# A transformer block on one core: the order of work on four engines and the order of users in a ring of seven PSUM banks are changed

## The chip, the cores and the metric

The kernel runs on one core of a Trainium2 chip. The metric is the device time of one execution, in microseconds. TensorE (PE), VectorE (DVE), ScalarE (ACT), GpSimd (POOL) and the DMA queue of SyncE (SP) run side by side and meet only at semaphores.

## The reference, cut to what matters

The input is 8 sequences of 256 tokens with 128 features. A stack of six layers runs twice with the same weights, with a selective-scan layer between the two. Everything is float32.

```
for i in range(6):
    x = attn_layer(shift_tokens(x), Wqkv[i], q_scale[i], k_scale[i], Wo[i]) + x
    x = ffn_layer(shift_tokens(x), ln_g[i], ln_b[i], W1[i], b1[i], W2[i], b2[i]) + x
```

attn_layer projects to queries, keys and values (16 heads of 64), divides queries and keys by their norms, rotates both (rotary tables), takes scores in windows of 32 queries against the 64 keys of the window and the one before it, adds a mask, takes the softmax, sums the values and projects back to 128 features. ffn_layer is a layer norm, a gated GELU layer with 341 hidden features, and a projection back.

## The kernel before, in words

**Items and steps.** The 8 sequences are 4 chunks of 2 (128 x 512 elements). An item is one chunk in one layer, so each stack has 24 items. An item is spread over some 29 steps, and a new item starts every 8 steps, so that about four items are always in work. A step takes one pair of heads of the newest item through its projections. Below, "step 0" to "step 7" means the step number modulo 8. Every engine walks the same list PLAN, and inside each step it does its own pieces in an order written out by hand (`tensor_stack`, `vector_stack`, `scalar_stack`, `gpsimd_stack`). An engine never looks ahead: what stands first waits, and the rest waits behind it.

**What falls where.** In every step: PE projects queries (L659 to L661, into "proj 0"), keys (the same lines, "proj 1") and the previous pair's values (L752 to L754); ACT squares queries and keys (L1096); DVE multiplies them by sine and cosine tables (L881, L886; "rotate 0" and "rotate 1") and turns the values (L902); SP moves the sine part across partitions; POOL adds it (L1270). In even steps, for one group of four heads: PE scores (L722, 128 small matmuls) and the spread of the inverse key norms (L741); ACT masks (L1148), key norms copied (L1154), exponents (L1173), attention output copied (L1166); DVE scaled scores (L951, one instruction for each of two sequences), sum (L963), reciprocal (L968), maximum (L957); POOL softmax division (L1290); PE the value product (L695, 128 small matmuls). In odd steps: POOL takes off the maximum (L1276) and scales (L1284); DVE turns the probabilities (L977). Once an item: first half of the output projection and gates in step 1 (L671, L762; DVE L915; norm work DVE L933, L935, L938 and then ACT L1132), value part of the hidden layer in steps 2 and 3 (L767, DVE L984), its projection in step 4 (L774, DVE L991), second half of the output projection in step 5 (L671, DVE L915), then the token shift on ACT (L1079, L1080), centering in step 6 (PE L637, ACT L1062, POOL L1248), variance in step 7 (PE L642, DVE L847). In step 6 the next item's tokens are split in a high and a low part (ACT L1111 xs_hi, DVE L908 xs_lo). At the end of a layer the next layer's weights are split pair by pair (ACT L1103, POOL L1295).

**The bank ring.** PE writes into 7 general PSUM banks that are handed out in turn by `Banks.use`. Each user waits until the reader of the bank's last user has signalled; as there are 7 banks, that is the user seven places earlier. One period of 8 steps has 63 uses, which is nine turns of the ring, so every item finds the same pattern. In an even step the uses before the change are: proj 0, spread, scores of sequence 0, scores of sequence 1, (a use of the once-an-item work), proj 1, four of the value product, v. The readers' signals are cos_q and cos_k (DVE L886), k_inv_kept (ACT L1154), k_norms_off (DVE L951), att_kept (ACT L1166), v_kept (DVE L902).

**Masks.** Scores are added onto a mask that is already in the bank. Where the bank's last user had written it whole, ACT copies the mask in; otherwise PE writes it with a matmul (L712):

```
if BANKS.filled[key]:
    w.wait_ge(S["mask_set"], MASKED[key])
else:
    pe_bank(w, key)
    e.matmul(g[seq][:, :], ident_bf[:, :], mask_bf[:, :], start=True, stop=False, skip_group_check=True)
```

The value product does not write its banks whole; the projections, v, the spread and the scores do.

## Time and profile before

| | |
|---|---|
| median of 3 runs | 3372.07 us (3358.28 to 3372.07) |
| the profiled execution's own time | 3364.97 us |
| its span | 3363.2 us |
| mean granted clock of TensorE | 0.946 of full speed |
| busy: PE / DVE / ACT / POOL | 86% / 87% / 61% / 72% of the span |

A row of a timeline gives start, duration, engine, line, operation, output<-inputs, and in brackets the engine's idle time before it and what released it. Rows of groups give count, busy time and mean duration, then idle time before them with the releasers. A busy PE is one whose matmuls are in flight, not one at its peak. "issue" is idle time in which the engine waited for nothing that the profile shows.

### The profile page before, as it was taken

The page shows a single profiled execution, that of the slowest core. Times are in us where ns is not written, and L with a number is a line of the kernel's source. Part 1 is how long each engine was busy: PE and PEld are TensorE (multiplying, and loading weights), DVE is VectorE, ACT ScalarE, POOL GpSimd, SP SyncE. Part 2 cuts the span into 40 slices and gives each one's busy share as a digit, 9 for nine tenths or more (in the row PEclk, how much of TensorE's full clock was granted, in tenths as well). Part 3 has the DMA queues.
Part 4 walks back from the last instruction along what each step waited for, and adds up shares of the span by engine and source line. Part 5 has one row for each costly group of instructions (what it writes and reads, how often), then busy time and mean ns, then how long its engine had stood idle before and what let it go on. Part 6 is the DMA issues. An engine that isn't in the chain of part 4 may idle for free. (4 is left out here: it accounts for less than half of the span.)

```text
span 3363.2 us, 132089 instructions
## 1 busy us (share of the span) xinstructions
PE 2891.1 (86%) x57914; PEld 1829.9 (54%) x57914; DVE 2933.3 (87%) x4224; ACT 2059.8 (61%) x3820; POOL 2423.5 (72%) x1679
## 2 busy tenths in 40 slices
PE   5689988988999989897677788999998989998987
PEld 3455555655666655553233455555565555555553
DVE  6789989999999988986898789889899989898984
ACT  3466666666676666665663566666566666566663
POOL 3678787787787787874464678778787787787773
PEclk8899999999999999998897899999999999999998
DMA  5233333333333333320002233333343333342330
GB/s 136 65 80 77 82 91 74 84 92 71 84 92 73 89 85 72 88 65 28 10 4 59 68 81 78 75 93 77 73 101 73 86 90 71 82 94 65 88 74 15
DMA packets 114726, 250.85 MB, mean 75 GB/s; under 512 B 27244, under 2 KB 60648, under 8 KB 114152
## 3 DMA queue, kind: packets, MB, share of 16 engines
q1 hardware_dynamic: 114152, 242.40, 30.5%
q8 instruction: 457, 7.49, 1.0%
q14 instruction: 117, 0.96, 0.1%
HBM read 37.82 MB, written 3.15 MB: 12 GB/s over the span
## 5 line engine op out<-in xcount | busy, mean ns | idle before, releaser
L1096 ACT ACTIVATE squares<-general 128x512 f32<-128x512 f32 x768 | 453.7, 597 | 716.8 <-PE general L661 707.8
L1290 POOL TENSOR_TENSOR probs<-probs,row_sum 128x1024 f32<-128x1024 f32 x192 | 365.4, 1903 | 442.4 <-DVE row_sum L968 442.3
L1270 POOL TENSOR_TENSOR q_ring<-q_ring,partner 128x512 f32<-128x512 f32 x384 | 491.0, 1279 | 203.9 <-DMA partner<-sines 203.3
L881 DVE TENSOR_TENSOR sines<-general,layer_tables 128x512 f32<-128x512 f32 x768 | 515.8, 672 | 85.3 <-ACT squares L1096 81.8
L1270 POOL TENSOR_TENSOR k_ring<-k_ring,partner 128x512 f32<-128x512 f32 x384 | 490.9, 1278 | 0.0
L695 PE MATMUL general<-probs_t,v_buf 32*64 32x64 f32 x24576 | 339.0, 234 | 153.8 <-issue 85.1
L659 PE MATMUL general<-xs_hi,wqkv_lo 128*128 128x512 f32 x768 | 454.2, 591 | 18.5 <-DVE xs_lo L908 8.0
L695 PEld LDWEIGHTS general<-probs_t,v_buf 32*64 32x64 f32 x24576 | 304.0, 134 | 246.1 <-issue 237.5
L1284 POOL TENSOR_TENSOR probs<-probs,q_scale 128x1024 f32<-128x1024 f32 x192 | 365.4, 1903 | 15.1
L722 PE MATMUL general<-k_ring,q_ring 64*32 64x64 f32 (+1 forms) x24576 | 295.3, 223 | 92.5 <-issue 53.1
L671 PE MATMUL general<-att,wo 128*128 128x512 f32 x768 | 366.2, 621 | 4.6 <-ACT att L1166 4.2
L1276 POOL TENSOR_TENSOR probs<-probs,row_max 128x1024 f32<-128x1024 f32 x192 | 366.7, 1910 | 0.0
L722 PEld LDWEIGHTS general<-k_ring,q_ring 64*32 64x32 f32 x24576 | 261.1, 105 | 126.8 <-issue 109.4
L661 PE MATMUL general<-xs_hi,wqkv_hi 128*128 128x512 f32 x768 | 313.1, 408 | 2.3 <-issue 2.2
L660 PE MATMUL general<-xs_lo,wqkv_hi 128*128 128x512 f32 x768 | 313.1, 408 | 1.9 <-issue 1.9
L659 PEld LDWEIGHTS general<-xs_hi,wqkv_lo 128*128 128x128 f32 x768 | 152.1, 198 | 267.9 <-issue 235.5
L1166 ACT ACTIVATE att<-general 128x256 f32<-128x256 f32 x768 | 231.4, 388 | 93.0 <-PE general L695 92.6
L902 DVE STREAM_TRANSPOSE v_buf<-general 128x512 f32<-128x512 f32 x384 | 264.8, 690 | 25.4 <-PE general L754 25.2
L733 PE MATMUL sums<-squares,consts 128*32 128x512 f32 x1536 | 249.0, 612 | 38.8 <-ACT squares L1096 36.5
L963 DVE TENSOR_REDUCE row_sum<-probs 128x16 f32<-128x1024 f32 x192 | 230.2, 1199 | 52.2 <-ACT probs L1173 51.8
L951 DVE TENSOR_TENSOR probs<-general,k_inv 128x512 f32<-128x512 f32 x384 | 244.8, 677 | 29.7 <-PE general L722 27.7
L752 PE MATMUL general<-xs_hi,wqkv_lo 128*128 128x256 f32 x768 | 258.7, 337 | 3.5 <-issue 3.5
(233 smaller groups left out, 6369.9 us busy)
## 6 DMA issues: line engine op xcount, KB each, us to landing
partner<-sines SPq DMA_DIRECT2D x1536, 128.0 KB, 2.3
wqkv_raw<-in_wqkv SPq DMA_DIRECT2D x80, 208.0 KB, 2.7
wo<-in_wo SPq DMA_DIRECT2D x12, 512.0 KB, 5.1
w<-in_w SPq DMA_DIRECT2D x12, 341.0 KB, 3.2
base_dram<-x SPq DMA_DIRECT2D x8, 256.0 KB, 2.4
att<-in_wqkv SPq DMA_DIRECT2D x2, 1024.0 KB, 6.7
sines<-base_dram SPq DMA_DIRECT2D x8, 256.0 KB, 3.9
w<-in_w SPq DMA_DIRECT2D x12, 128.0 KB
```

The source lines that it names most:

```text
L659: e.matmul(g[:, :], wqkv_lo[:, p, cut], xs_hi[:, r, :], start=True, stop=False)
L660: e.matmul(g[:, :], wqkv_hi[:, p, cut], xs_lo[:, r, :], start=False, stop=False)
L661: e.matmul(g[:, :], wqkv_hi[:, p, cut], xs_hi[:, r, :], start=False, stop=True)\
L671: done = e.matmul(g[:, :], wo[:, p, :], att[:, p, :], start=(p == OUT_PAIRS[i][0]), stop=(p == OUT_PAIRS[i][-1]))
L695: done = e.matmul(o, lhs, rhs, start=(kb == 0), stop=True, skip_group_check=True)
L722: done = e.matmul(o, qw, kw, start=False, stop=True, skip_group_check=True)
L881: e.tensor_tensor(by_seq(sines[:, i % 2, which, :]), g, both(layer_tables[:, 2 * which + 1, :]), ALU.mult).then_inc(S[f"sin_{side}"], 1)
L1096: e.activation(squares[:, (2 * p + which) % 4, :], general_of(("proj", k, n, p, which))[:, :], ACT.Square).then_inc(S[f"squared_{side}"], 1)
L1270: e.tensor_tensor(y, y, partner[:, i % 2, which, :], ALU.add).then_inc(S[f"rotated_{side}"], 1)
L1276: e.tensor_tensor(y, y, spread_keys(row_max[:, i % 2, :]), ALU.subtract).then_inc(S["max_off"], 1)
L1284: e.tensor_tensor(y, y, spread_keys(q_scale8[:, n % 2, group, :]), ALU.mult).then_inc(S["q_norms_off"], 1)
L1290: e.tensor_tensor(y, y, spread_keys(row_sum[:, i % 2, :]), ALU.mult).then_inc(S["probs_done"], 1)
```

## The change

No arithmetic is added or removed. The lags become plain numbers with the same values. What moves:

- **Ring and PE, even steps:** the uses are now proj 0, scores 0, scores 1, spread; on PE the spread stands between the two halves of the scores (windows 0 to 3 and 4 to 7). First half of the output projection and variance also stand ahead of the scores in the text, but they fall in odd steps, which have no scores.
- **Ring and PE, step 4:** the keys' projection (proj 1) now comes before the hidden layer's output projection. The same holds for the entering norms of the first items. The value product's halves are no longer separated by the second output projection, which falls in an odd step.
- **DVE:** the turn of the probabilities ahead of rotate 1 (odd steps); in step 1 the addition of the first output half (L915) ahead of the norm work (L933, L935, L938).
- **ACT:** weight splitting (L1103) to the front of the step; layer-norm root ahead of the queries' squares (step 0); exponents ahead of the keys' squares (even steps); in step 6 the centering copy (L1062) ahead of the token split (L1111).
- **POOL:** the softmax division behind the second addition of the rotary parts.
- Separate names in `Step` for the pieces on different engines, with the same step numbers as before.

```
 # Banks.stack
-            if st.spread:
-                n, group = st.spread
-                self.use(("spread", k, n, group), "k_inv_kept", (g + n) * GROUPS + group + 1)
...
             if st.scores:
                 n, group = st.scores
                 for seq in range(CHUNK_SEQS):
                     self.use(("scores", k, n, group, seq), "k_norms_off", ((g + n) * GROUPS + group) * 2 + seq + 1)
...
+            if st.spread:
+                n, group = st.spread
+                self.use(("spread", k, n, group), "k_inv_kept", (g + n) * GROUPS + group + 1)
```

```
 # tensor_stack
                 if st.now:
                     pe_project(e, w, k, *st.now, 0)
...
+                if st.scores:
+                    pe_scores(e, w, k, *st.scores, range(0, NWIN // 2))
                 if st.spread:
                     pe_spread(e, w, k, *st.spread)
-                if st.out_first:
-                    pe_out(e, w, k, *st.out_first)
-                if st.scores:
-                    pe_scores(e, w, k, *st.scores, range(0, NWIN // 2))
...
-                if st.ffn_out is not None:
-                    pe_ffn_out(e, w, k, st.ffn_out)
...
+                if st.now:
+                    pe_project(e, w, k, *st.now, 1)
+                if st.ffn_out is not None:
+                    pe_ffn_out(e, w, k, st.ffn_out)
                 if st.enter:
                     pe_enter(e, w, k, *st.enter)
-                if st.now:
-                    pe_project(e, w, k, *st.now, 1)
```

```
 # vector_stack
-                if st.norms_back is not None:
-                    dve_norms_back(e, w, k, st.norms_back)
...
-                if st.out_first:
-                    dve_out(e, w, k, *st.out_first)
+                if st.first_added is not None:
+                    dve_out(e, w, k, st.first_added, 0)
...
+                if st.norms_back is not None:
+                    dve_norms_back(e, w, k, st.norms_back)
+                if st.turn:
+                    dve_turn(e, w, k, *st.turn)
                 if st.now:
                     dve_rotate(e, w, k, *st.now, 1)
-                if st.turn:
-                    dve_turn(e, w, k, *st.turn)
```

```
 # scalar_stack
+                if st.exps:
+                    act_exp(e, w, k, *st.exps)
...
-                if st.split is not None:
-                    act_split_tokens(e, w, k, st.split)
...
                 if st.center is not None:
                     act_center(e, w, ("ffn", k, st.center))
+                if st.split is not None:
+                    act_split_tokens(e, w, k, st.split)
...
                 if st.now:
                     act_square(e, w, k, *st.now, 1)
-                if st.exps:
-                    act_exp(e, w, k, *st.exps)
```

```
 # gpsimd_stack
-                if st.exps:
-                    pool_probs(e, w, k, *st.exps)
                 if st.enter:
                     pool_enter(e, w, k, *st.enter)
                 if st.added:
                     pool_rotate(e, w, k, *st.added, 1)
+                if st.probs:
+                    pool_probs(e, w, k, *st.probs)
```

## Rows read from the trace of the kernel before

**Rows 1.** Windows: length, busy us (instructions) by engine, TensorE clock, DMA share, GB/s

```profile
400.00:1300.00 900.00, 814.64 (x17666) 530.76 (x17664) 823.52 (x1201) 581.58 (x1100) 706.41 (x488) 0.98 0.36 83
1094.00:1154.00 60.00, 56.51 (x1207) 36.21 (x1205) 56.91 (x84) 39.67 (x75) 48.24 (x33) 1.00 0.39 93
839.00:842.00 3.00, 3.00 (x8) 1.92 (x8) 2.42 (x4) 0.60 (x1) 1.49 (x1) 0.53 0.22 52
```

**Rows 2.** Groups by line: busy us, mean ns, idle before and its releasers

```profile
L902 DVE STREAM_TRANSPOSE v_buf<-general 128x512 f32<-128x512 f32 x384 | 264.8, 690 | 25.4 <-PE general L754 25.2
...
L963 DVE TENSOR_REDUCE row_sum<-probs 128x16 f32<-128x1024 f32 x192 | 230.2, 1199 | 52.2 <-ACT probs L1173 51.8
...
L1295 POOL TENSOR_TENSOR wqkv_lo<-wqkv_raw,wqkv_hi 128x416 fp32r<-128x416 f32 x80 | 87.9, 1099 | 57.3 <-ACT wqkv_hi L1103 57.3
...
L915 DVE TENSOR_TENSOR x<-x,general 128x512 f32<-128x512 f32 x96 | 64.2, 669 | 68.5 <-PE general L671 68.5
...
L712 PE MATMUL general<-mask_bf,ident_bf 128*128 128x512 bf16 x18 | 6.0, 386 | 0.0
```

**Rows 3.** Source line L991, once an item: count, first and last start

```profile
L991 DVE SCALAR_TENSOR_TENSOR x<-general,vec,x x19: 724/729/751, 299.5 to 1397.9; 128x512 f32<-128x512 f32 x19
```

**Rows 4.** Timeline of DVE over one undisturbed item: its two second output additions bound it

```profile
1097.11 0.69 DVE L915 TENSOR_TENSOR x<-x,general 128x512 f32<-128x512 f32 x1 [1.18 <-PE general L671]
...
1103.30 0.68 DVE L908 TENSOR_TENSOR xs_lo<-xs,xs_hi 128x512 fp32r<-128x512 f32 x1
1104.33 0.69 DVE L881 TENSOR_TENSOR sines<-general,layer_tables 128x512 f32<-128x512 f32 x1 [0.35 <-ACT squares L1096]
...
1132.71 1.27 DVE L951 TENSOR_TENSOR probs<-general,k_inv 128x512 f32<-128x512 f32 x2
...
1136.19 1.22 DVE L963 TENSOR_REDUCE row_sum<-probs 128x16 f32<-128x1024 f32 x1 [0.36 <-ACT probs L1173]
...
1154.60 0.69 DVE L915 TENSOR_TENSOR x<-x,general 128x512 f32<-128x512 f32 x1 [1.16 <-PE general L671]
```

**Rows 5.** Timeline of PE, same item

```profile
1100.39 1.53 PE L722 MATMUL general<-k_ring,q_ring 64*32 64x32 f32 x128 [0.48 <-ACT general L1148]
...
1111.40 0.39 PE L741 MATMUL general<-inv_parts,spread_sel 128*128 128x256 f32 x2
1111.73 1.46 PE L722 MATMUL general<-k_ring,q_ring 64*32 64x32 f32 x128
...
1115.44 0.41 PE L695 MATMUL general<-probs_t,v_buf 32*64 32x64 f32 x19 [1.35 <-DVE q_ring L886]
...
1129.91 1.49 PE L722 MATMUL general<-k_ring,q_ring 64*32 64x32 f32 x128 [0.53 <-ACT general L1148]
...
1133.53 1.23 PE L695 MATMUL general<-probs_t,v_buf 32*64 32x64 f32 x94 [0.37 <-DVE probs L951]
```

**Rows 6.** Timeline of ACT, same item

```profile
1099.12 1.12 ACT L1148 ACTIVATE general<-mask_bf 128x512 f32<-128x512 bf16 x2
...
1101.24 0.63 ACT L1111 ACTIVATE xs_hi<-xs 128x512 fp32r<-128x512 f32 x1
1103.01 0.60 ACT L1062 ACTIVATE centered<-general 128x512 f32<-128x512 f32 x1 [1.14 <-PE general L637]
...
1128.13 0.63 ACT L1132 ACTIVATE inv_parts<-k_inv 128x512 fp32r<-128x512 f32 x1 [1.07 <-DVE k_inv L938]
```

**Rows 7.** Timeline of POOL, same item, steps 6 and 2

```profile
1103.68 1.19 POOL L1248 TENSOR_TENSOR rstd<-centered 128x512 f32<-128x512 f32 x1 [0.49 <-ACT centered L1062]
...
1135.12 1.29 POOL L1270 TENSOR_TENSOR q_ring<-q_ring,partner 128x512 f32<-128x512 f32 x1 [3.46 <-DMA partner<-sines]
```

**Rows 8.** Timeline of DVE in step 6 of an item at a layer's end

```profile
982.69 1.81 DVE L908 TENSOR_TENSOR xs_lo<-xs,xs_hi 128x512 fp32r<-128x512 f32 x1
```

**Rows 9.** Timeline of POOL at the same time

```profile
982.68 1.28 POOL L1270 TENSOR_TENSOR k_ring<-k_ring,partner 128x512 f32<-128x512 f32 x1
```

**Rows 10.** Timeline of PE in step 2 of an earlier, disturbed item

```profile
838.34 0.35 PE L753 MATMUL general<-xs_lo,wqkv_hi 128*128 128x256 f32 x1 [2.15 <-issue]
```

More of the change, by code:

```diff
@@ L34 @@
 POOL_BANKS = 7
[L37 to L45 removed]
+SCORES_LAG = 10
+SCORES_REST_LAG = 10
+SCALE_LAG = 10
+OFF_LAG = 11
+EXP_LAG = 12
+PROBS_LAG = 12
+TURN_LAG = 13
+VALUES_LAG = 14
+VALUES_REST_LAG = 14
+KEPT_LAG = 14
 V_LAG = 1
[L47 removed]
+SPREAD_LAG = 10
 PROBS = 2
@@ L108, in __init__ @@
         self.exps = self.group(t, EXP_LAG)
+        self.probs = self.group(t, PROBS_LAG)
         self.turn = self.group(t, TURN_LAG)
@@ L275, in stack @@
                 self.use(("proj", k, n, p, 0), "cos_q", (g + n) * PAIRS + p + 1)
-            if st.spread:
-                n, group = st.spread
-                self.use(("spread", k, n, group), "k_inv_kept", (g + n) * GROUPS + group + 1)
-            if st.out_first:
-                n, i = st.out_first
-                self.use(("project", k, n, i), "att_added", (g + n) * 2 + i + 1)
+            if st.out_first is not None:
+                self.use(("project", k, st.out_first, 0), "att_added", (g + st.out_first) * 2 + 1)
+            if st.var is not None:
+                self.var(("ffn", k, st.var))
             if st.scores:
@@ L285, in stack @@
                     self.use(("scores", k, n, group, seq), "k_norms_off", ((g + n) * GROUPS + group) * 2 + seq + 1)
-            if st.var is not None:
-                self.var(("ffn", k, st.var))
+            if st.spread:
+                n, group = st.spread
+                self.use(("spread", k, n, group), "k_inv_kept", (g + n) * GROUPS + group + 1)
             if st.center is not None:
                 self.norm(("ffn", k, st.center))
-            if st.ffn_out is not None:
-                self.use(("ffn_out", k, st.ffn_out), "ffn_added", g + st.ffn_out + 1)
             if st.gates is not None:
@@ L298, in stack @@
                     self.use(("value", k, n, j), "hidden_done", (g + n) * 3 + j + 1)
+            if st.now:
+                n, p = st.now
+                self.use(("proj", k, n, p, 1), "cos_k", (g + n) * PAIRS + p + 1)
+            if st.ffn_out is not None:
+                self.use(("ffn_out", k, st.ffn_out), "ffn_added", g + st.ffn_out + 1)
             if st.enter and st.enter[1] == 0:
@@ L302, in stack @@
                 self.var(("enter", k, st.enter[0]))
-            if st.now:
-                n, p = st.now
-                self.use(("proj", k, n, p, 1), "cos_k", (g + n) * PAIRS + p + 1)
             if st.values:
```

99 lines of the change are left out of this document (49 added, 50 removed).

## The prediction, made before the changed kernel had run

> **What bounds the kernel now.** I read the windows first. In the steady stretch from 400 to 1300 us DVE is busy 823.5 of 900 us and PE 814.6, while POOL (706) and ACT (582) have room [rows 1]. No single engine is the bound: DVE and PE each have about 9% idle time, and the question is who makes whom wait. An item comes every (1397.9 - 299.5) / 18 = 61.0 us [rows 3]. Items without a disturbance are shorter: from one second output addition to the next it is 1154.60 - 1097.11 = 57.5 us [rows 4], at a full clock [rows 1]. The other 3.5 us are stalls of PE that the profile gives to nothing, such as 2.15 us in [rows 10], and the stretches of lower clock behind them [rows 1].
>
> The timelines of the undisturbed item show that the path changes engine twice an item. In step 5 DVE waits 1.18 and, an item later, 1.16 us for PE's second half of the output projection [rows 4]; all items together wait 68.5 us there, 48 second halves, 1.43 each [rows 2]. So PE is late at that point in every item. Going back along PE, it works without a wait worth naming to the value product of step 2, which starts at 1133.53, 0.14 us after the first of DVE's two scaled-score instructions ends (1132.71 + 0.68 = 1133.39), and which the trace puts down to it [rows 5]. This is the ring: the fourth bank of that product is the one in which the scores of sequence 0 stood, seven uses before. From there back, the path is on DVE to the output addition in step 5, with no idle over 0.2 us but the 0.35 at 1104.33. One item is thus a **DVE leg** (step 5 to step 2) and a **PE leg** (step 2 to step 5). What shortens a wait of DVE inside the PE leg gains nothing; DVE waits longer in step 5 instead. That holds for the 0.36 us before the row sum at 1136.19 [rows 4] and for most of the 51.8 us before all row sums [rows 2].
>
> **The change part by part, in us an item.**
>
> *Gate of the value product.* In an even step the uses before were proj 0, spread, scores 0, scores 1; in step 2 the fourth bank of the product came from scores 0, the third from the spread. With the spread behind the scores the same two banks come from scores 1 and scores 0. The product must now wait for DVE's second scaled-score instruction: 1133.98 instead of 1133.39. That moves the start of the PE leg by **0.6**. In step 0 there is no once-an-item use in between, and the gate moves from cos_q (the 1.35 us wait at 1115.44, [rows 5]) to the first scaled scores, again 0.6 later. In an undisturbed item PE has slack behind it (it waits 0.53 for masks at 1129.91); in a disturbed item, where PE arrives late at step 2, this one counts instead. So 0.6 either way; bounds 0 and 1.2.
>
> *Centering copy ahead of the token split, step 6.* ACT made xs_hi at 1101.24, while it waited 1.14 us for PE's centering [rows 6], and DVE could make xs_lo at 1103.30 and go on at 1104.33 [rows 4]. Now ACT first waits: centered 1103.01 to 1103.61, xs_hi to about 1104.25, then xs_lo (0.68) on DVE, with the second rotation queued behind it, and behind that the row sum, the values' turn and the whole DVE leg. The rotation starts near 1104.9 instead of 1104.33. Two things move it. PE's centering comes about 0.1 earlier: the wait of 0.48 for two masks [rows 5] is nearly gone, since here one mask becomes a PE matmul, but the spread (0.33) and that matmul (6.0 / 18 = 0.33, [rows 2]) come in. Against it stands POOL: its square runs from 1103.68 to 1104.87 [rows 7], over the new place of xs_lo. Where xs_lo began together with a POOL addition it took 1.81 us instead of 0.68 [rows 8, 9], the addition's 1.28 and its own work. If that holds here, the rotation starts near 1105.4. So 0.5 or 1.0. In disturbed items DVE waits for PE later in the step anyway (25.2 us before L902, [rows 2]) and takes up a part. I take **0.7**; bounds 0.2 and 1.1.
>
> The Trainium skill ("SBUF — State Buffer", "SBUF: two separate sides") says that a VectorE instruction with both inputs in SBUF and a GpSimd instruction that reads SBUF exclude each other for a whole instruction, whoever starts first. Rows 8 and 9 agree. By it alone the term would be 1.0 and the time some 13 us more; the chosen value stands between.
>
> *Spread inside the scores.* PE changes between the full array and small tiles twice more a group. The spread takes 0.33 us from its start to that of the scores [rows 5], with one change in it; nothing shows a change alone, so it costs between 0 and 0.33, and as the two matmuls must take the larger part, about 0.1. One group (step 4) lies in the PE leg: **0.2**; bounds 0 and 0.66.
>
> *Output addition ahead of the norm work, step 1.* inv_parts (1128.13, [rows 6]) comes 0.65 later, behind it the masks and scores of step 2 (1129.91), and the spread is no longer done in that wait. PE then reaches the value product of step 2 some 1.1 later: it had 0.37 to spare [rows 5] and gets 0.6 more from the new gate. **0.1**; bounds 0 and 0.5.
>
> *The rest, taken at nothing.* Keys' projection ahead of the hidden output (step 4): both stand in the PE leg, in the other order; DVE adds the hidden output before it rotates, so its start differs by 0.3 at most, covered by the 1.16 wait in step 5. Exponents ahead of the keys' squares: ACT mostly idles there, and the exponents' input is a step old; in step 0 a table load and the exponents now stand before the squares, while DVE still has the turn of the root to do; where that cover is too short, DVE's second rotation starts late, by 0 to the 0.69 of its first instruction [rows 4]. Turn ahead of rotate 1: the sum is the same, but the sine part of the keys is 1.23 later in odd steps, so SP's four transfers too, and POOL's next addition, which waited 3.46 for them already [rows 7] with nothing of the path behind it. Division behind the second addition on POOL: it waited for DVE's reciprocal anyway, and the turn that needs it is a step later. Masks: about 92 fewer on ACT, as many matmuls on PE at 0.33, in steps 6 (counted) and 0 (PE has the 1.35 wait). Weight splits at the front of ACT's step: POOL waited 57.3 us for 16 of them [rows 2], beside the path mostly; I give it **-5 us in all**, bounds -20 and 5.
>
> *Sum.* 0.6 + 0.7 + 0.2 + 0.1 = 1.6 an item. Of 48 items about 42 have full neighbours: 67 us, less 5. The profiled execution took 3364.97 (span 3363.2), which gives 3427; the runs' median is 7 us above it, and I forecast **3430**.
>
> **Rivals.**
>
> *Faster: DVE alone sets the pace.* If the output wait in step 5 were made by DVE's own lateness, each wait taken from DVE would count, first the 51.8 us before the row sums: 3365 - 52 = 3313. For it: DVE is busy longer than PE. Against it: the 1.43 us in every item, and the value product pinned to DVE 0.14 us behind. It decides if that wait in step 5 shrinks under about 0.3 us while step 2 starts no later. 0.19.
>
> *No change.* The disturbances (3.5 us an item) hide the 0.6 and the 0.7 instead of adding to them, as where DVE waits for PE's values. 3355 to 3388, at 3372. For it: 27 such waits. Against it: a stall of PE inside the PE leg adds to a later start. 0.14.
>
> *Slower still: the clock.* PE's wait of 1.35 before the value product of step 0 grows by 0.6, and by what DVE loses in step 6, to about 2.7 us. Behind a gap of 2.15 [rows 10] the granted clock was 0.53, which is the lower level of 1.2 GHz [rows 1], while in the undisturbed item, gaps of 1.35 included, it was 1.00. The 3 us window at 0.53 did about 1.4 us less work than one at 2.4 GHz; with some 0.3 to 0.5 of it taken up by PE's slack, 1.1 more for 42 items: 3430 + 46 = 3476. 0.15. The Trainium skill ("TensorE: Matmul & The Clock Gate", "HAM oscillation — how this bites in real kernels") warns that idle gaps between groups of matmuls put the clock back down; that is this rival.
>
> **How the numbers follow.** The forecast has 0.52; its own range from the terms' bounds is 3385 to 3475. The rivals have 0.19, 0.14 and 0.15. A measurement of this kernel can tell about 0.5%, 17 us. Faster: 0.20, same 0.14, slower 0.66. The range 3345 to 3480 leaves out most of the faster rival (0.13) and the upper part of the clock rival (0.07).
>
> **What would show it.** (1) The value product of steps 2, 4 and 6 starts no earlier than the second L951 of its step, that of step 0 no earlier than the first. (2) In step 6 xs_lo starts only behind the centering copy, at times with a duration above 0.68, and the keys' sine after it starts 0.5 to 1 later. (3) The row sum waits for the exponents almost never, and the wait in step 5 before L915 grows from 1.2 to about 1.7. (4) L712 rises to some 110, L1148 falls to some 274. (5) POOL's wait before L1295 is gone. I am wrong if an undisturbed item takes under 58 us, most likely because DVE's earlier row sums carry through to step 5, or if the clock falls in step 0.

## The result, and the profile after

The changed kernel takes 3424.01 us (median of 4 runs, 3416.67 to 3424.89) where the kernel before takes 3371.48 in the same session: a ratio of 1.0161, 95% interval 1.0132 to 1.0189. The forecast was 3430. The profiled execution has a span of 3422.9 us, 59.7 more than before.

Where those 59.7 us are is seen in one line that stands once an item. The addition of the hidden output to x, 24 times a stack, first and last start (L991 before, L1000 after). The kernel before, first stack, then second:

```profile
L991 DVE SCALAR_TENSOR_TENSOR x<-general,vec,x x24: 724/732/751, 235.7 to 1644.6; 128x512 f32<-128x512 f32 x24
L991 DVE SCALAR_TENSOR_TENSOR x<-general,vec,x x24: 723/728/751, 2007.1 to 3357.6; 128x512 f32<-128x512 f32 x24
```

The changed kernel, first stack, second stack, and last the stretch that answers to [rows 3]:

```profile
L1000 DVE SCALAR_TENSOR_TENSOR x<-general,vec,x x24: 734/751/752, 217.2 to 1680.3; 128x512 f32<-128x512 f32 x24
L1000 DVE SCALAR_TENSOR_TENSOR x<-general,vec,x x24: 750/751/752, 2024.9 to 3417.3; 128x512 f32<-128x512 f32 x24
L1000 DVE SCALAR_TENSOR_TENSOR x<-general,vec,x x19: 750/751/752, 281.3 to 1424.6; 128x512 f32<-128x512 f32 x19
```

The first of them comes 18.5 us **earlier**. The 23 items behind it take 54.2 us more. From the last of stack 0 to the first of stack 1 it is 344.6 us instead of 362.5, so 17.9 less, and then 41.9 more. The sum is -18.5 + 54.2 - 17.9 + 41.9 = 59.7. So the steady part lost 96 us and the fillings of the pipeline gained 36. The item takes (1424.6 - 281.3) / 18 = 63.5 us instead of 61.0. The shortest item, from one second output addition to the next, takes 60.0 us instead of 57.5. The prediction had 1.6 for the item and nothing for the start.

The windows of the changed kernel: the stretch of the first line of [rows 1], one item, and three microseconds behind the value product of step 0 in it:

```profile
400.00:1300.00 900.00, 816.24 (x16950) 521.11 (x16949) 803.00 (x1153) 548.82 (x1032) 683.33 (x471) 0.95 0.34 80
805.00:866.00 61.00, 56.07 (x1168) 35.84 (x1154) 55.62 (x81) 37.49 (x71) 43.61 (x30) 0.97 0.31 71
823.00:826.00 3.00, 3.00 (x67) 2.81 (x54) 2.93 (x5) 1.21 (x4) 2.83 (x3) 0.50 0.32 72
```

DVE does 48 instructions fewer in the same 900 us, PE 716 fewer. The groups that answer to [rows 2], and those of the small operations that turn out to matter, in the changed kernel:

```profile
L911 DVE STREAM_TRANSPOSE v_buf<-general 128x512 f32<-128x512 f32 x384 | 268.5, 699 | 30.5 <-PE general L763 30.3
L972 DVE TENSOR_REDUCE row_sum<-probs 128x16 f32<-128x1024 f32 x192 | 229.5, 1195 | 6.0 <-ACT probs L1182 6.0
L924 DVE TENSOR_TENSOR x<-x,general 128x512 f32<-128x512 f32 x96 | 65.7, 684 | 103.9 <-PE general L680 103.8
L858 DVE TENSOR_SCALAR norm_t<-norm_t 128x16 f32<-128x16 f32 x56 | 52.2, 932 | 1.9
L917 DVE TENSOR_TENSOR xs_lo<-xs,xs_hi 128x512 fp32r<-128x512 f32 x48 | 50.9, 1061 | 39.1 <-ACT xs_hi L1120 39.1
L1000 DVE SCALAR_TENSOR_TENSOR x<-general,vec,x 128x512 f32<-128x512 f32 x48 | 36.0, 751 | 69.3 <-PE general L783 69.3
L704 PE MATMUL general<-probs_t,v_buf 32*64 32x64 f32 x24576 | 345.7, 244 | 199.5 <-DVE probs L960 124.9 <-issue 69.1 <-DVE v_buf L911 3.3
L1304 POOL TENSOR_TENSOR wqkv_lo<-wqkv_raw,wqkv_hi 128x416 fp32r<-128x416 f32 x80 | 90.6, 1133 | 8.0 <-ACT wqkv_hi L1112 8.0
L721 PE MATMUL general<-mask_bf,ident_bf 128*128 128x512 bf16 x110 | 41.6, 390 | 7.0 <-ACT general L1157 7.0
```

The same four groups in the kernel before:

```profile
L849 DVE TENSOR_SCALAR norm_t<-norm_t 128x16 f32<-128x16 f32 x56 | 20.4, 364 | 1.9
L908 DVE TENSOR_TENSOR xs_lo<-xs,xs_hi 128x512 fp32r<-128x512 f32 x48 | 43.1, 897 | 0.0
L991 DVE SCALAR_TENSOR_TENSOR x<-general,vec,x 128x512 f32<-128x512 f32 x48 | 35.4, 737 | 31.3 <-PE general L774 31.1
L695 PE MATMUL general<-probs_t,v_buf 32*64 32x64 f32 x24576 | 339.0, 234 | 153.8 <-issue 85.1 <-DVE q_ring L886 53.2 <-DVE probs L951 6.4
```

The row sums no longer wait (51.8 to 6.0). The output additions wait 35 us more, but not where the prediction had it: 21 of the 35 lie before the first halves in step 1, which never waited before. Before the second half in step 5 the wait is 1.13 us in the median instead of 1.16, and 1.36 in the mean instead of 1.13. The value product waits for the scaled scores and no longer for the cosine, and 121.9 of these 124.9 us lie in step 0. From the views of line L695 before and L704 after, what the product waited for, us and times:

```profile
  DVE q_ring L886: 53.2, 33
  DVE probs L951: 6.4, 17
```

```profile
  DVE probs L960: 124.9, 46
```

The split of the tokens waits for ACT, which it never did. And **L858**, an in-place addition to 16 numbers a partition, takes 932 ns instead of 364. The prediction did not name it.

**Step 7, where it shows.** Timeline of DVE in step 7 of one item of the changed kernel:

```profile
815.13 0.70 DVE L856 STREAM_TRANSPOSE norm_t<-general 128x512 f32<-128x512 f32 x1
815.87 0.95 DVE L858 TENSOR_SCALAR norm_t<-norm_t 128x16 f32<-128x16 f32 x1
816.86 0.26 DVE L860 RECIPROCAL norm_t<-norm_t 128x16 f32<-128x16 f32 x1
```

Timeline of POOL at the same time, and in step 1 of the next item:

```profile
814.88 1.90 POOL L1285 TENSOR_TENSOR probs<-probs,row_max 128x1024 f32<-128x1024 f32 x1
816.86 1.91 POOL L1293 TENSOR_TENSOR probs<-probs,q_scale 128x1024 f32<-128x1024 f32 x1
...
830.04 1.90 POOL L1285 TENSOR_TENSOR probs<-probs,row_max 128x1024 f32<-128x1024 f32 x1
832.02 1.91 POOL L1293 TENSOR_TENSOR probs<-probs,q_scale 128x1024 f32<-128x1024 f32 x1
```

DVE in that step 1:

```profile
830.88 1.15 DVE L942 CAST norm_t<-norm_t 128x128 fp32r<-128x128 f32 x1
832.06 2.01 DVE L944 TENSOR_TENSOR norm_t<-norm_t 128x128 f32<-128x128 f32 x1
```

POOL's subtraction ends at 816.78 and L858 at 816.82; the next pair ends at 831.94 and L942 at 832.03; the one after at 833.93 and L944 at 834.07. Each of the three DVE operations ends just behind a POOL operation that was running when it began. In the kernel before, POOL had its second rotary addition first in these steps and the subtraction started 1.2 us later. The reciprocal L860 starts together with the next POOL operation and takes 0.26 all the same, and the transposition L856 runs under the subtraction in 0.70. So it is certain forms of operation that are shut out. The views by line, durations in ns (min/median/max), the addition before, then the addition and the reciprocal after:

```profile
L849 DVE TENSOR_SCALAR norm_t<-norm_t x56: 181/334/1566, 18.8 to 3342.3; 128x16 f32<-128x16 f32 x56
L858 DVE TENSOR_SCALAR norm_t<-norm_t x56: 182/956/1434, 18.4 to 3402.3; 128x16 f32<-128x16 f32 x56
L860 DVE RECIPROCAL norm_t<-norm_t x56: 255/256/259, 18.6 to 3402.5; 128x16 f32<-128x16 f32 x56
```

In both traces the four additions that met no POOL operation took 0.18 us. All 47 that began under the subtraction in the changed kernel ended 0.04 us behind it. In the kernel before, 44 began under a rotary addition and ended 0.04 us behind that, so the 0.33 there was partly such a wait too. L944 is held in both kernels (1832 ns in the mean before, 1784 after): what changed for it is the POOL operation behind which it ends, the scaling instead of the subtraction. The Trainium skill ("SBUF — State Buffer", "SBUF: two separate sides") says that a VectorE instruction that has two SBUF inputs and a GpSimd instruction that reads SBUF exclude each other for a whole instruction, and so do a VectorE instruction in a mode that uses two ports and a GpSimd instruction. The three rows of L858, L942 and L944 fit it; that L858 and L942, with one tensor input, are in such a mode is not shown by any row.

**Steps.** A step is here the time between two queries' sines (L881, L890). Medians over the 38 items with full neighbours in both stacks, in us; then the mean item (over the 36 of them that are followed by such an item), and the time that the first three items take together, in the first stack and in the second. Each row is one profiled execution. All experiments are listed, for use below.

| | 0 | 1 | 2 | 3 | 4 | 5 | 6 | 7 | mean item | first three |
|---|---|---|---|---|---|---|---|---|---|---|
| before | 9.21 | 8.42 | 8.50 | 5.46 | 7.60 | 6.22 | 7.87 | 5.37 | 61.3 | 171.4, 169.3 |
| changed | 9.18 | 8.56 | 8.19 | 5.46 | 8.77 | 5.98 | 8.64 | 5.98 | 63.4 | 153.5, 150.8 |
| split_first | 9.19 | 8.57 | 8.19 | 5.46 | 8.72 | 5.98 | 7.90 | 6.00 | 62.7 | 153.8, 154.0 |
| division_between | 9.20 | 7.88 | 8.20 | 5.46 | 8.80 | 5.98 | 8.69 | 5.37 | 61.8 | 163.3, 162.3 |
| spread_first | 9.19 | 8.56 | 7.72 | 5.46 | 8.45 | 6.19 | 8.60 | 5.99 | 62.4 | 156.6, 155.2 |
| norms_first | 9.19 | 9.16 | 8.01 | 5.46 | 8.92 | 5.98 | 8.63 | 5.99 | 63.4 | 156.4, 150.9 |
| turn_back | 9.19 | 8.57 | 7.90 | 5.46 | 8.72 | 5.98 | 8.63 | 5.98 | 62.9 | 155.9, 154.2 |
| ffn_first | 9.20 | 8.57 | 8.03 | 5.46 | 8.83 | 6.00 | 8.65 | 5.99 | 63.5 | 154.4, 154.0 |
| no_epsilon | 9.21 | 8.56 | 8.19 | 5.46 | 8.72 | 5.98 | 8.64 | 4.99 | 62.1 | 154.9, 153.3 |
| before, exps_early | 9.21 | 8.42 | 7.29 | 5.46 | 8.45 | 6.22 | 7.69 | 5.37 | 61.0 | 168.4, 165.2 |
| before, division_last | 9.20 | 9.16 | 8.47 | 5.46 | 7.50 | 6.22 | 7.77 | 5.99 | 62.2 | 160.5, 157.9 |
| three_back | 9.21 | 7.83 | 7.90 | 5.46 | 8.40 | 6.19 | 7.77 | 5.37 | 61.1 | 161.3, 160.6 |
| three_back_start | 9.21 | 7.83 | 7.71 | 5.46 | 8.44 | 6.19 | 7.88 | 5.37 | 61.3 | 157.1, 153.2 |
| three_back_start_ffn | 9.21 | 7.83 | 7.78 | 5.46 | 8.44 | 6.22 | 7.80 | 5.37 | 61.1 | 155.3, 153.1 |

### The profile page after: what moved, and what is told of

Its sections match the earlier page's. It is cut to its first block, busy times and chain, and to the rows that moved or that the text cites. A ratio compares the mean times of both kernels' runs of the same rounds, so it can differ in the third digit from the quotient of the medians.

```text
span 3422.9 us, 132096 instructions
## 1 busy us (share of the span) xinstructions
PE 2988.4 (87%) x58006; PEld 1860.0 (54%) x58006; DVE 2978.5 (87%) x4224; ACT 2020.2 (59%) x3728; POOL 2428.4 (71%) x1679
## 4 chain that ended last, share of the span: by engine, by line
PE 57%; DVE 24%; issue 9%; ACT 5%; POOL 2%; DMA 1%; SPq 1%; DVEq 0%; POOLq 0%; ACTq 0%
PE general L680 8%; PE general L704 7%; PE general L731 7%; PE general L668 4%; PE sums L742 4%; PE general L776 4%; PE general L783 4%; PE general L669 3%; PE general L670 3%; DVE sines L890 3%; PE general L761 3%; PE general L771 2%; PE general L750 2%; PE general L762 2%; DVE q_ring L895 2%
## 5 line engine op out<-in xcount | busy, mean ns | idle before, releaser
L890 DVE TENSOR_TENSOR sines<-general,layer_tables 128x512 f32<-128x512 f32 x768 | 512.3, 667 | 61.0 <-ACT squares L1105 57.6
L704 PE MATMUL general<-probs_t,v_buf 32*64 32x64 f32 x24576 | 345.7, 244 | 199.5 <-DVE probs L960 124.9
L704 PEld LDWEIGHTS general<-probs_t,v_buf 32*64 32x64 f32 x24576 | 313.4, 142 | 308.7 <-issue 306.2
L668 PE MATMUL general<-xs_hi,wqkv_lo 128*128 128x512 f32 x768 | 438.6, 571 | 16.3 <-DVE xs_lo L917 7.6
L731 PE MATMUL general<-k_ring,q_ring 64*32 64x64 f32 (+1 forms) x24576 | 330.4, 223 | 43.1 <-issue 22.3
L761 PE MATMUL general<-xs_hi,wqkv_lo 128*128 128x256 f32 x768 | 273.1, 356 | 5.7 <-issue 5.5
L895 DVE TENSOR_TENSOR q_ring<-general,layer_tables 128x512 f32<-128x512 f32 x384 | 259.8, 677 | 0.0
```

The source lines that it names most:

```text
L668: e.matmul(g[:, :], wqkv_lo[:, p, cut], xs_hi[:, r, :], start=True, stop=False)
L704: done = e.matmul(o, lhs, rhs, start=(kb == 0), stop=True, skip_group_check=True)
L731: done = e.matmul(o, qw, kw, start=False, stop=True, skip_group_check=True)
L761: e.matmul(g[:, cut], wqkv_lo[:, p, cols], xs_hi[:, r, cut], start=seq == 0, stop=False, skip_group_check=True)
L890: e.tensor_tensor(by_seq(sines[:, i % 2, which, :]), g, both(layer_tables[:, 2 * which + 1, :]), ALU.mult).then_inc(S[f"sin_{side}"], 1)
```

## The experiments

All times are given as ratios to the kernel before on the same chip and in the same session; 0.1% is 3.4 us. The changed kernel's own ratio, 1.0161, is from the first session, so that a difference to it is known to some 0.4% (14 us), and the error of 1.0161 is in every such difference. The kernel before had a median of 3371.48 us in that session and of 3359.66, 3357.31 and 3368.96 in the later ones. Unless it says "before", an experiment is the changed kernel with one edit.

**Token split ahead of the centering copy (split_first).**

```
+ if st.split is not None: act_split_tokens(...)
  if st.center is not None: act_center(...)
- if st.split is not None: act_split_tokens(...)
```

> The changed kernel with one order put back: ScalarE makes the rounded tokens ahead of the centering copy again (step 6). In the trace of the changed kernel the keys' sine of step 6 starts 4.54 us into the step against 3.43 before, and the token split of VectorE lasts 1.11 us, under GpSimd's square. Theory (every delay of VectorE between step 5 and step 2 is on the path): step 6 gets back 0.7 to 1.1 us, times 42 items, so 29 to 46 us faster than the changed kernel: 3378 to 3395, ratio to the kernel before 1.002 to 1.007. Rival (disturbances or another engine take the item's end anyway): the time stays at 3424, ratio 1.015, with the sine earlier all the same.

Measured: 1.0094 (1.0062 to 1.0126), 23 us faster than the changed kernel's 1.0161. Step 6 is back to 7.90, and the split, in the groups of this kernel, is no longer stretched or waited for:

```profile
L917 DVE TENSOR_TENSOR xs_lo<-xs,xs_hi 128x512 fp32r<-128x512 f32 x48 | 33.9, 706 | 5.3 <-ACT xs_hi L1120 5.2
```

The gain is clear of the rival's nothing, and under the theory's 29 to 46 us. The delay of step 6 is on the path.

**Division between the two rotary additions (division_between).**

```
  pool_rotate(..., 0)
+ if st.probs: pool_probs(...)
  if st.enter: pool_enter(...)
  pool_rotate(..., 1)
- if st.probs: pool_probs(...)
```

> The changed kernel with GpSimd's division of the probabilities back between its two rotary additions, ahead of its part of the entering norm. In the changed kernel GpSimd's subtraction of the row maximum starts 0.94 us into step 7 instead of 2.17 and VectorE's small addition of the variance lasts 0.95 us instead of 0.33 under it; step 7 grew from 5.37 to 5.98 us. Theory A (the earlier subtraction blocks VectorE, and step 7 is in the VectorE leg): the small addition is back at 0.33, step 7 at about 5.4, 0.6 x 42 = 25 us faster, ratio about 1.008. Part of it may be lost again in the first items of each stack, where the changed kernel gained some 18 us a stack: if the place of the division behind the entering norm is what gave that, the first three items lose up to 36 us together and the time is no shorter, ratio 1.016 to 1.02. Rival B (step 7 grew for another reason): no change in step 7, ratio 1.016.

Measured: 1.0076 (1.0049 to 1.0102), 29 us faster. Step 7 gave 0.61 as theory A said, and step 1 gave 0.68, which it did not say. Against that the first three items lost 9.8 and 11.5 us. The small operations of step 7 on DVE, then the groups of the two that the subtraction had stretched, in this kernel:

```profile
802.72 0.34 DVE L858 TENSOR_SCALAR norm_t<-norm_t 128x16 f32<-128x16 f32 x1
803.09 0.26 DVE L860 RECIPROCAL norm_t<-norm_t 128x16 f32<-128x16 f32 x1
```

```profile
L858 DVE TENSOR_SCALAR norm_t<-norm_t 128x16 f32<-128x16 f32 x56 | 20.4, 365 | 1.9
L942 DVE CAST norm_t<-norm_t 128x128 fp32r<-128x128 f32 x48 | 31.0, 647 | 3.6 <-ACT norm_t L1135 3.4
```

**Spread ahead of the scores (spread_first).**

```
  pe_project(..., 0)
+ if st.spread: pe_spread(...)
  pe_out(..., 0); pe_var(...); pe_scores(..., range(0, NWIN // 2))
- if st.spread: pe_spread(...)
  pe_scores(..., range(NWIN // 2, NWIN))
```

with the same move in Banks.

> The changed kernel with the spread ahead of the scores (and of the first half of the output projection) again, on TensorE and in the ring of banks. Theory: the bank gate of the value products goes back from the second to the first scaled-score instruction (0.6 us earlier in steps 2, 4 and 6, and to the queries' cosine in step 0), and the two changes between full array and small tiles vanish (0.2): 0.8 us of an item, 30 to 35 us, ratio 1.005 to 1.008. Rival (PE's slack behind the gate takes the 0.6, so that only the 0.2 shows): 8 us, ratio 1.013. Rival (the gate matters more, since it also brings the low clock behind the wait of step 0): 50 us or more, ratio about 1.00, and the granted clock of the whole run back at 0.946 from 0.932.

Measured: 1.0069 (1.0040 to 1.0099), 31 us faster, inside the theory's range. Steps 2 and 4 fall by 0.47 and 0.32, step 5 rises by 0.21. Where in those steps it lies is another matter than the theory had it. The product of step 2 starts 2.66 us into the step instead of 2.69, so hardly earlier; the keys' sine of that step, whose projection PE makes ahead of the product, starts 3.40 us into it instead of 3.73. In step 4 the product starts at 3.39 instead of 3.74, and the hidden output ahead of it is earlier by as much. The value product waits for the cosine again:

```profile
L704 PE MATMUL general<-probs_t,v_buf 32*64 32x64 f32 x24576 | 346.3, 241 | 186.0 <-DVE q_ring L895 97.6 <-issue 80.8 <-DVE v_buf L911 4.2
```

The last rival fell in both halves: 31 us and not 50, and the clock of the run stays at 0.936.

**The kernel before, exponents early alone (exps_early).**

```
  act_norms(...)
+ if st.exps: act_exp(...)
  ...
  act_square(..., 1)
- if st.exps: act_exp(...)
```

> The kernel before with one edit alone: ScalarE's exponents ahead of the rest of its step (behind the norms), so ahead of the keys' squares. Theory (the waits that VectorE has before its row sums, 52 us in all, lie mostly inside TensorE's leg and are given back in the wait of step 5; but steps 6 and 0 are in VectorE's own leg): -15 to +5 us, ratio 0.996 to 1.002, the row-sum wait almost gone and the wait before the second output addition up from 68.5 us. Rival (VectorE alone sets the pace): 52 us faster, ratio 0.985. Rival (the table load and the exponents ahead of the keys' squares delay the second rotation): 10 to 25 us slower, ratio 1.003 to 1.007.

Measured: 0.9941 (0.9908 to 0.9975), 20 us faster, a little more than the theory's range and far from the 52. Step 2 loses 1.21 us, and step 4 takes back 0.85. Of the 44 us that the row sums no longer wait, 21 reappear before the sines, which wait for the squares of PE's projections, and 4 each before the output additions and the additions of the hidden output (31.3 to 35.4). The sines' group in the kernel before:

```profile
L881 DVE TENSOR_TENSOR sines<-general,layer_tables 128x512 f32<-128x512 f32 x768 | 515.8, 672 | 85.3 <-ACT squares L1096 81.8 <-DMA partner<-sines 1.2
```

The groups of this kernel:

```profile
L881 DVE TENSOR_TENSOR sines<-general,layer_tables 128x512 f32<-128x512 f32 x768 | 517.5, 674 | 105.9 <-ACT squares L1096 101.5 <-DMA partner<-sines 0.6
L963 DVE TENSOR_REDUCE row_sum<-probs 128x16 f32<-128x1024 f32 x192 | 229.8, 1197 | 7.6 <-ACT probs L1173 7.5
L915 DVE TENSOR_TENSOR x<-x,general 128x512 f32<-128x512 f32 x96 | 64.2, 669 | 72.8 <-PE general L671 72.8
```

**The three orders back together (three_back).**

> The changed kernel with three orders put back together: the token split ahead of the centering copy on ScalarE, GpSimd's division between its two rotary additions, the spread ahead of the scores. Alone they gave ratios to the kernel before of 1.0094, 1.0076 and 1.0069, from 1.0161: 0.67%, 0.85% and 0.92% each. Theory (VectorE's leg and TensorE's leg follow one another in every item, so what is taken from either adds up): the sum, 2.4%, ratio 0.992 (3335 us where the kernel before takes 3362), an item of 60.1 us in the steady part. Rival (they cover one another: once VectorE is early, TensorE's leg or its disturbances set the time, or the reverse): not below 1.000, an item of 61.3 us or more. The long wait of the second output addition tells them apart: by the theory it stays near 1.4 us an item.

Measured: 0.9924 (0.9892 to 0.9955), 2.4% under the changed kernel, the sum of the three. That sum holds the error of 1.0161 three times and is known to 1% only, so it excludes the rival (not below 1.000) but cannot show that the three add up in full. The medians of the steps add up as well: 0.7 (split) + 1.2 (division) + 0.6 (spread) is 2.5, and the sum over the steps falls from 60.76 to 58.13, 2.6. But the mean item is 61.1, not 60.1: of the 3.3 us that it lost in the three single runs, 2.3 came. In part that is made up in the first items, where the three together lose 7.8 and 9.8 us and the single runs sum to 13 and 19. The wait of the second output addition, by which the two theories were to be told apart, has a mean of 1.13 us in step 5, as in the kernel before, against 1.36 in the changed kernel. What disturbs the items in this kernel I did not separate.

**The kernel before, division last alone (division_last).** The reverse of the second experiment, on the other kernel.

> The kernel before with one edit alone: GpSimd's division of the probabilities behind its second rotary addition. Theory (the subtraction of the row maximum starts 1.2 us earlier in the odd steps and shuts VectorE's small two-input or in-buffer operations out while it runs): step 7 +0.6 us (the variance's small addition 0.95 instead of 0.33) and step 1 +0.6 us (in the norm work, an operation that read 0.5 to 1.0 takes 1 to 2), 1.2 x 42 = 50 us slower in the steady part, less up to 20 in the first three items of each stack: ratio 1.009 to 1.015. Rival (the division's place costs only together with the other edits): 1.000, steps 7 and 1 at 5.37 and 8.42 us as before.

Measured: 1.0095 (1.0057 to 1.0133), 32 us slower. Step 7 is at 5.99, step 1 at 9.16. This one edit has the two signs of the whole: an item 0.9 longer and the first three items 10.9 and 11.4 us shorter. The groups of this kernel:

```profile
L849 DVE TENSOR_SCALAR norm_t<-norm_t 128x16 f32<-128x16 f32 x56 | 53.7, 959 | 1.9
L933 DVE CAST norm_t<-norm_t 128x128 fp32r<-128x128 f32 x48 | 66.9, 1394 | 25.3 <-ACT norm_t L1126 25.3
```

**Norm work ahead of the first output addition (norms_first)**, on DVE: the call of dve_norms_back back in front of the output addition.

> The changed kernel with VectorE's norm work (three operations, step 1) ahead of the first output addition again. The prediction costed this edit at 0.1 us an item. In the trace of the changed kernel the addition waits up to 3.2 us for TensorE's first half in the disturbed items, with the norm work queued behind it; in undisturbed items it does not wait. Theory (that wait is now in VectorE's leg): with the norm work ahead the wait is filled, 1 to 2 us in a third of the items, 15 to 30 us faster than the changed kernel, ratio 1.007 to 1.012. Rival (the addition later means the second half, the scores of step 2 and the gate behind them are no earlier, so nothing comes of it): 1.015 to 1.018.

Measured: 1.0205 (1.0178 to 1.0232). The gain that the theory forecast did not come. Against the changed kernel's 1.0161 this is 0.44% more, at the edge of the 0.4% to which such a difference is known, and the times themselves (3422.15 against 3424.01) and the mean items (63.4 in both) are equal. So no difference between the two kernels is shown. Step 1 is 9.16 instead of 8.56, and step 2 behind it is shorter, 8.01 instead of 8.19. The wait of the output addition did shrink, but the norm work now waits for ACT's root, and its operations begin nearer to the start of POOL's subtraction:

```profile
L942 DVE CAST norm_t<-norm_t 128x128 fp32r<-128x128 f32 x48 | 59.3, 1235 | 33.0 <-ACT norm_t L1135 32.6
L944 DVE TENSOR_TENSOR norm_t<-norm_t 128x128 f32<-128x128 f32 x48 | 90.3, 1881 | 1.7
L924 DVE TENSOR_TENSOR x<-x,general 128x512 f32<-128x512 f32 x96 | 64.2, 669 | 75.1 <-PE general L680 75.1
```

The output addition, which reads a PSUM bank, keeps its time under the subtraction (676 to 689 ns in all 96 of the changed kernel), so it is the better one to have there for step 1; for the whole item nothing is gained.

**Turn behind the second rotation (turn_back)**, on DVE.

> The changed kernel with VectorE's turn of the probabilities behind the second rotation again. The prediction took this edit at nothing: the same work in both orders, only the keys' sine 1.2 us later with the turn ahead. Theory: ratio 1.014 to 1.018, as the changed kernel, with GpSimd's second addition starting 1 us earlier and no step of VectorE shorter. Rival (the later sine, the four transfers behind it and GpSimd's addition push the rest of GpSimd's step, and so the subtraction and scaling that the exponents wait for): 10 to 25 us faster, ratio 1.009 to 1.013. The other side (the turn earlier lets the value products start earlier): slower, ratio 1.02 or more.

Measured: 1.0146 (1.0113 to 1.0180). The interval holds the changed kernel's ratio, as the theory has it, and also the end of the rival's range (1.013); the mean item is 62.9 instead of 63.4. No difference is shown, and one of 10 us is not excluded.

**Hidden output ahead of the keys' projection (ffn_first)**, on PE and in Banks.

> The changed kernel with TensorE's hidden output ahead of the keys' projection again (step 4), on TensorE and in the ring of banks. The prediction took this order at nothing. In the changed kernel step 4 grew from 8.1 and 7.4 us (medians of the two stacks) to 8.8 and 8.7, and VectorE's addition of the hidden output, now behind both projections, waits for TensorE 69 us in all against 31. Theory (both stand in TensorE's leg, so the order only moves the wait between steps 4 and 5): step 4 0.4 shorter, step 5 longer by as much, ratio 1.013 to 1.018. Rival (the late hidden output holds VectorE's second rotation, which the values and the output projection do not need, but the steps behind do): 0.5 us an item, 21 us faster, ratio 1.008 to 1.012.

Measured: 1.0166 (1.0138 to 1.0195): nothing. The total is as the theory had it, the steps are not: step 4 did not get shorter (8.83 against 8.77) nor step 5 longer. The hidden output's addition waits 41.7 us instead of 69.3, but the sines of step 4 now wait for their squares instead, 27.7 us against 3.4, and the output additions still wait 104.0:

```profile
L1000 DVE SCALAR_TENSOR_TENSOR x<-general,vec,x 128x512 f32<-128x512 f32 x48 | 36.0, 749 | 41.7 <-PE general L783 41.4
```

**Without the small addition (no_epsilon).** The constant 1e-5 is not added to the variances.

```
- e.tensor_scalar(var_t[:, :, 0:1], var_t[:, :, 0:1], EPS, None, ALU.add)...
- w.wait_ge(S["ln_var_turned"], i + 1)
```

> The changed kernel without VectorE's small addition to the variance (128x16x1, in place): the 1e-5 that the reference adds to each variance is left out, nothing else. In step 7 of the changed kernel that addition lasts 0.95 us, to 0.04 us past the end of GpSimd's subtraction, and 0.33 in the kernel before, where the subtraction begins later. Theory (GpSimd's running operation shuts out this form of VectorE operation, but not the reciprocal behind it, which reads and writes the same buffer): with the addition gone all of the 0.95 goes, step 7 falls from 5.98 to about 5.0 us, 1.0 x 42 = 42 us faster than the changed kernel, ratio 1.003 to 1.006. Rival (any VectorE operation on this buffer waits for GpSimd's): the reciprocal takes the wait over, step 7 falls by 0.1 to 0.35, ratio 1.012 to 1.016.

Measured: 1.0018 (0.9997 to 1.0039), 48 us faster than the changed kernel. Step 7 is at 4.99, as the theory had it, and the total is a little better than its range. Of these 48, the 0.57 us an item by which the operation was stretched against the kernel before are 24, and the 0.36 that it took there already are 15; the other 9 are within the error. DVE in step 7 of this kernel (its lines behind the edit are two lower):

```profile
803.67 0.70 DVE L856 STREAM_TRANSPOSE norm_t<-general 128x512 f32<-128x512 f32 x1
804.40 0.26 DVE L858 RECIPROCAL norm_t<-norm_t 128x16 f32<-128x16 f32 x1
```

POOL at the same time:

```profile
803.42 1.91 POOL L1283 TENSOR_TENSOR probs<-probs,row_max 128x1024 f32<-128x1024 f32 x1
```

The reciprocal, on the same 16 numbers of the same buffer, runs right inside POOL's subtraction at its own 0.26. With the 255 to 259 ns that all 56 reciprocals of the changed kernel take, this shows that it is the form of the operation that is shut out, not the buffer.

**Best of both (three_back_start and three_back_start_ffn).** The three orders back, and the division last only where it gained:

```
+ if st.probs and st.t >= 24: pool_probs(...)
  if st.enter: pool_enter(...)
  pool_rotate(..., 1)
+ if st.probs and st.t < 24: pool_probs(...)
```

> The kernel with the three orders put back (ratio 0.9924), but in the first 24 steps of each stack (three items) GpSimd's division stays behind its second rotary addition, as in the changed kernel. With the division last these three items took 153.5 and 150.8 us in the changed kernel, 163.3 and 162.3 with the division alone put back, 161.3 and 160.6 with all three. Theory (the place of the division gives that difference, through what stands behind it on GpSimd's queue in those items): the first three items back to some 152 us, the steady part unchanged, 16 to 19 us faster than with the three put back, ratio 0.986 to 0.988. Rival (the gain of the start needs the other orders of the changed kernel too): 0.992, the first three items at 160 us or more.

> The previous kernel with TensorE's hidden output ahead of the keys' projection as well, so that of the steady part's edits only the exponents ahead of the squares, the turn ahead of the second rotation, the output addition ahead of the norm work and the entering norm's place remain. Theory (the order of the hidden output only moves a wait from step 4 to step 5): within 0.3% of the previous kernel. Rival (it holds VectorE's second rotation in the path): 0.4 to 0.8% faster than the previous kernel, ratio 0.98.

Measured: 0.9893 (0.9864 to 0.9922) and 0.9878 (0.9847 to 0.9910). The first items are at 157.1 and 153.2, so about 6 us a stack came back of the expected 8 or 9, and 0.3% of the expected 0.5%. By the ratio alone the rival's 0.992 would stand; it is the first items, forecast by it at 160 or more, that exclude it. The hidden output's order adds 0.15%, within error. The last one, 3323.27 us, is 1.2% under the kernel before and 2.8% under the changed one.

## Why the prediction was right, and where it was right by luck

**The model of the path held in its totals.** What is put into either leg shows in the item (split_first, spread_first). What is taken out of DVE inside the PE leg is given back for the larger part (exps_early: 1.21 in step 2, 0.85 back in step 4). The order of two pieces of the PE leg is worth nothing (ffn_first). Its picture of step 2 did not hold, as the next term shows.

**Gate of the value product (0.6) and spread inside the scores (0.2).** The sum is right: 0.8 forecast; 31 us over 42 items is 0.74, the mean item says 1.0. The two were not tried apart, and the traces speak against the split. In the kernel before, PE waited in step 2 for the first scaled scores in 17 of 38 items. In the changed kernel it waits there for the second in none: PE is still busy, and the product starts 0.22 us or more behind their end. Most of what spread_first gave back in steps 2 and 4 lies ahead of the product. So the step "The product must now wait for DVE's second scaled-score instruction", with its 0.6 at the start of the PE leg, is not what the runs show; what they show is a PE that comes later to the product. How much of that the spread between the halves of the scores makes, beyond the 0.3 us in those two steps, stays open. Point (1) of what would show it came out so, but only as a bound. The gate itself shows in step 0. There the product starts 2.00 us into the step in the median instead of 1.54, 0.14 us behind the end of this DVE row's first instruction (821.79), and PE has room for it:

```profile
821.11 1.27 DVE L960 TENSOR_TENSOR probs<-general,k_inv 128x512 f32<-128x512 f32 x2
```

```profile
821.93 1.91 PE L704 MATMUL general<-probs_t,v_buf 32*64 32x64 f32 x128 [2.18 <-DVE probs L960]
```

**Centering copy (0.7).** Right: 23 us over 42 is 0.55, the medians of step 6 say 0.74. Point (2) came out: the split lasts 1061 ns in the mean, a clash with POOL's square that lies between the two values that the prediction weighed, and the keys' sine of step 6 starts 4.47 us into the step instead of 3.42.

**Output addition ahead of the norm work (0.1).** With the rest of the change in place no effect on the time is shown (norms_first). Step 1 is 0.6 us shorter by it, which the term did not have: it looked only at when inv_parts comes and not at what POOL runs beside the norm work. The later PE that it did have is there: the product of step 2 starts 2.69 us into the step with the edit and 2.59 without.

**Division behind the second addition (nothing).** This is the step of the prediction that failed: "it waited for DVE's reciprocal anyway, and the turn that needs it is a step later". That looked at who waits for the division, not at what is queued behind it on POOL. With the second rotary addition already done, the subtraction of the next step starts 1.2 us earlier, onto L858 in step 7 and L942 in step 1, and L944 then ends with the scaling. Measured: 1.6 us an item in the changed kernel, 0.9 in the kernel before. The prediction cited the very rule for the token split and did not ask it of this move.

**Exponents early (nothing).** Mis-sized: 20 us faster alone, which is 0.3 an item and 3 to 4 us a stack at the start.

**Start of the stacks (nothing).** Missed altogether: 36 us gained. The division last gives 11 us a stack of it, and exponents early 3 to 4 (step table); the other 3 or so were not tracked down. The weight splits, given -5, were not tried alone; that POOL's wait is nearly gone (57.3 to 8.0) is point (5).

**The sum.** 1.6 us an item was forecast and 2.1 to 2.5 came, and 36 us of start gain were taken off. Each of the four that matter, made or undone alone and with its start, gave: spread and gate 31 us, centering copy 23, division 29, exponents -20. Together that is 63, against the 62 that the forecast added up and the 54 of the ratio. The two terms that were put at nothing, 29 and -20, nearly cancel. The 3430 against 3424 is therefore closer than the working deserved. The range has a flaw of its own: the terms' bounds, added up, are 0.2 to 3.5 us an item and give 3360 to 3522 us, not the 3385 to 3475 that the prediction has from them.

**The rivals.** *Faster*: what was to decide it was the wait in step 5 shrinking under 0.3, and it is 1.13 in the median; exps_early alone gave 20 of the 52. The second half of point (3), that this wait grows from 1.2 to about 1.7, failed as well. Its first half, the row sums, held. *No change*: the terms were not hidden (split_first, spread_first). *The clock*: its mechanism came, and the prediction had called itself wrong if it did. Behind the 2.18 us wait of the row above, the clock is 0.50, the lower level of 1.2 GHz, for 823 to 826; in the kernel before, the item of [rows 5] with its 1.35 kept 1.00. The second and third matmul of the first projection behind that product follow one another by over 0.33 us (0.42 in this item, 0.23 at the full clock) in 27 of 38 items, against 9 before. Its price was not measured, since no run held the clock. In the changed kernel step 1 has a mean of 9.20 us in the 27 items and of 8.56 in the other 11, but the whole item is no longer in the 27 (63.0 against 63.8). In division_between the gate is the same and 14 of 38 items are slow. PE's idle time before and in the product of step 0, in the median, is 3.0 us in the changed kernel, 2.3 in division_between and 1.6 in the kernel before, so the gate alone does not make it. Point (4) held: 110 mask matmuls as forecast, and on ACT 274.

## What to carry to other kernels

When an instruction is moved, look at what its engine does earlier because of it, and lay that beside the engine whose operations were seen to lengthen under it: most of the cost of the division stood in no wait of any view, only in longer durations, first that of a 16-element addition. Compare mean durations by group between two traces as carefully as idle times. And cost the filling of a pipeline apart from its steady part: the same edit can have opposite signs in the two, and can then be made in one of them alone.

## What was not expected of the hardware

A small DVE operation, 128x16 in place, took 0.95 us instead of 0.33, and 0.18 where POOL was idle, with no wait shown. When it began under a POOL operation it ended some 0.04 us behind that operation's end. A cast of 128x128 (0.23 alone, up to 1.8 here) ended 0.08 behind, and a two-input subtraction of 128x128 (0.29 alone, 2.01 here) 0.15 behind. A reciprocal of the same 128x16 (0.26) and transpositions were not touched.
